# Scores and output projection of an attention and expert layer as plain fp32 products instead of three reduced ones

## What is computed

```python
# layer 0: attention, 16 heads of 64, one key/value head shared by all
xn = ln(x, g_norm)
q  = l2norm(heads(xn @ Wq)) * q_scale
k  = l2norm(concat([null_k, (xn @ Wkv)[..., :64]])) * k_scale
v  = concat([null_v, (xn @ Wkv)[..., 64:]])
sim  = einsum('bhid,bjd->bhij', q, k) * 8 + rel_pos_bias    # causal and mask
out  = einsum('bhij,bjd->bhid', softmax(sim), v)
x1   = x + ln(out.reshape(b, n, 1024) @ Wout, g_out)
# layer 1: 8 experts of width 128 (top 2) and a shared one of width 256
y = x1 + sum_k w_k * (leaky(x1 @ Wg_e) * (x1 @ Wu_e)) @ Wd_e + shared(x1)
```

## Time and profile before

| | before |
|---|---|
| time, median of 3 runs | 1070.17 us (1069.21 to 1070.3) |
| profiled execution | 1068.73 us, span 1066.9 us, mean TensorE clock 0.998 |
| TensorE busy | 1011.4 us (95%) |
| VectorE busy | 725.8 us (68%) |
| ScalarE busy | 541.0 us (51%) |
| GpSimd busy | 438.6 us (41%) |

### The profile page before, as it was taken

How to read it: one execution, slowest core, us unless ns; L and a number is a source line. 1 busy time by engine, 2 the same in 40 slices (tenths; PEclk the granted TensorE clock), 3 DMA queues, 4 the chain that set the end, 5 groups by cost and what they waited for, 6 DMA issues and landing times.

```text
span 1066.9 us, 22567 instructions
## 1 busy us (share of the span) xinstructions
PE 1011.4 (95%) x7300; PEld 823.6 (77%) x7300; DVE 725.8 (68%) x2497; ACT 541.0 (51%) x1596; POOL 438.6 (41%) x422
## 2 busy tenths in 40 slices
PE   3877999999999999999999999999999999999998
PEld 2765877878787887878777787787878788787877
DVE  8889487665867558665677647766586755866543
ACT  3598256652565435663456515665256643566220
POOL 1644254441454333642535515444145433354212
PEclk9999999999999999999999999999999999999999
DMA  5326423111132013311132212311113210221043
GB/s 198 73 77 209 138 69 121 51 60 62 61 110 89 36 47 100 100 61 61 42 114 77 69 42 72 119 49 62 62 61 110 89 37 29 96 103 62 36 133 105
DMA packets 41004, 87.79 MB, mean 82 GB/s; under 512 B 4193, under 2 KB 19041, under 8 KB 40625
## 3 DMA queue, kind: packets, MB, share of 16 engines
q1 hardware_dynamic: 39920, 83.57, 23.9%
q10 hardware_dynamic: 960, 2.62, 0.7%
HBM read 76.57 MB, written 9.60 MB: 81 GB/s over the span
## 4 chain that ended last, share of the span: by engine, by line
PE 70%; DVE 15%; issue 6%; ACT 3%; DVEq 0%; POOL 0%; ACTq 0%; POOLq 0%
PE psY L1647 13%; PE psS L1517 6%; PE psO L1553 5%; PE psG L71 5%; PE psG L69 5%; PE psG L70 5%; PE psT L1528 5%; PE psS L1512 3%; PE psS L69 2%; PE psS L71 2%; PE psS L70 2%; PE psT L1535 2%; PE psO L1556 2%; DVE work L423 2%; PE psT L69 2%
## 5 line engine op out<-in xcount | busy, mean ns | idle before, releaser
L592 POOL TENSOR_TENSOR work<-work,rden 128x514 f32<-128x514 f32 x128 | 134.2, 1049 | 328.6 <-DVE rden L1143 328.1
L1647 PE MATMUL psY<-Wd,H 128*128 128x256 f32 x640 | 171.7, 397 | 0.0
L757 ACT ACTIVATE work<-work,low 128x257 f32<-128x257 f32 x256 | 128.5, 504 | 63.5 <-DVE low L1161 63.5
L69 PE MATMUL psG<-x1T_hi,Wgu 128*128 128x512 f32 (+1 forms) x292 | 134.6, 461 | 3.5 <-ACT leaky L801 1.9
L1647 PEld LDWEIGHTS psY<-Wd,H 128*128 128x128 f32 x640 | 111.6, 189 | 28.1 <-issue 14.4
L1161 DVE CUSTOM_DVE_ANT_0 work<-psS,bias,null_s 128x256 f32<-128x256 f32 x256 | 113.1, 478 | 22.3 <-PE psS L1517 19.4
L1257 DVE SCALAR_TENSOR_TENSOR leaky<-leaky 128x512 f32<-128x512 f32 x80 | 55.4, 692 | 93.3 <-ACT leaky L801 93.3
L71 PE MATMUL psG<-x1T_lo,Wgu 128*128 128x512 f32 (+1 forms) x292 | 114.7, 393 | 0.0
L70 PE MATMUL psG<-x1T_hi,Wgu 128*128 128x512 f32 (+1 forms) x292 | 113.7, 389 | 0.0
L581 POOL TENSOR_TENSOR rq<-qss,neghalf 128x16 f32<-128x16 f32 x32 | 97.5, 3049 | 34.4 <-DVE qss L1137 34.4
L761 ACT ACTIVATE work<-work,low 128x129 f32<-128x129 f32 x256 | 99.4, 390 | 0.0
(11 more groups left out here) (264 smaller groups left out, 2567.6 us busy)
## 6 DMA issues: line engine op xcount, KB each, us to landing
Wgu<-wexp SPq DMA_DIRECT2D x80, 512.0 KB, 3.4
Wb<-wscr SPq DMA_DIRECT2D x64, 256.0 KB, 3.6
wexp<-Wgu SPq DMA_DIRECT2D x10, 512.0 KB, 2.9
xres<-in_x SPq DMA_DIRECT2D x8, 512.0 KB, 4.0
xin<-in_x SPq DMA_DIRECT2D x7, 512.0 KB, 4.1
out<-work SPq DMA_DIRECT2D x7, 512.0 KB, 3.2
H<-in_wgu SPq DMA_DIRECT2D x10, 256.0 KB, 3.5
bias<-bscr SPq DMA_DIRECT2D x4, 512.0 KB, 6.2
```

The costliest lines, as they stand in the source:

```text
L69: te.matmul(dst, a_hi, b_hi, start=start, stop=False)
L592: pool.tensor_tensor(T1[sl][:, hs, :], T1[sl][:, hs, :], rden[sl][:, 1, hs].unsqueeze(2) .to_broadcast([P, 2, N + 1]), ALU.mult)
L757: act.activation(T1[sl][:, h, :], T1[sl][:, h, :], ACT.Exp, scale=-1.0, bias=low[sl][:, 1, h:h + 1], accum_out=den[sl][:, 1, h:h + 1])
L1647: mm = te.matmul(psY[:, t // 2, (t % 2) * D:(t % 2 + 1) * D], H[:, k % H_RING, t * P:(t + 1) * P], Wd[:, ORDER[k], :], start=(k == 0 and t ...
```

## The change

Scores and the output projection become plain fp32 products. Queries, keys, head outputs and output weights are kept in one fp32 part each. The subtractions of the low parts go (`KB_lo`, `qT_lo` of queries and of head outputs, `wout_trail`), and so do the copies to `Wout_hi`. Of the eight units of turned queries ScalarE copies the even ones and VectorE the odd ones. The output weights are loaded straight to their place, and the residual of round 0 is loaded at the start, ahead of the down weights. The value product waits for ScalarE's copy (`o_lead`).

```diff
-        Wout = [sb(f"Wout_{part}", [P, PAIRS, D], F32R) for part in PARTS]
+        Wout = sb("Wout", [P, PAIRS, D])
-        KB = [sb(f"KB_{part}", [P, BB, N], F32R) for part in PARTS]
+        KB = sb("KB", [P, BB, N])
-        qT = [sb(f"qT_{part}", [P, PAIRS, TOK], F32R) for part in PARTS]
+        qT = sb("qT", [P, PAIRS, TOK])
...
+        def turned_q(eng, r, n):
+
+            t, half = n // 2, n % 2
+            need(eng, qT_ps, r, n + 1)
+            dst = qT[:, 4 * half:4 * half + 4, t * P:(t + 1) * P]
+            src = q_bank(n).rearrange("p (q i) -> p q i", q=4)
+            if half == 0:
+                eng.activation(dst, src, ACT.Copy).then_inc(qT_a.sem, 1)
+            else:
+                eng.tensor_copy(dst, src).then_inc(qT_v.sem, 1)
...
             sp.wait_ge(pre_v.sem, V_MASK)
-            load_mask(0)
+            load_round(0)
             sp.dma_start(Wd[:], wdown).then_inc(ld_down.sem, 16)
...
-            sp.wait_ge(pre_v.sem, V_WOUT)
-            sp.dma_start(xres[:], x_t[0]).then_inc(xres_in.sem, 16)
...
-            for half in range(2):
-                act.dma_start(Wout_in[half], wout[:, half * 4:half * 4 + 4, :]).then_inc(ld_out.sem, 16)
+            act.dma_start(Wout[:], wout).then_inc(ld_out.sem, 16)
...
-                for n in range(4):
-                    turned_q(r, n)
+                for n in (0, 2):
+                    turned_q(act, r, n)
...
-                    if moe is None and n in WOUT_AT:
-                        half = n - WOUT_AT[0]
-                        act.activation(Wout[0][:, half * 4:half * 4 + 4, :], Wout_in[half], ACT.Copy) \
-                            .then_inc(w_lead.sem, 1)
...
-                need(dve, kdT_ps, r, 1)
-                need(dve, kb_a, r, 1)
-                dve.tensor_tensor(KB[1][:, :, :], psO[:, :].rearrange("p (b j) -> p b j", b=BB),
-                                  KB[0][:, :, :].bitcast(F32), ALU.subtract).then_inc(kb_v.sem, 1)
...
-                for n in range(4):
-                    turned_q(r, n)
-                    if n == 0 and moe is not None:
-                        hidden(moe, 1)
-                    if n == 1 and moe is not None:
-                        router_weights(moe)
+                if moe is not None:
+                    hidden(moe, 1)
+                turned_q(dve, r, 1)
+                if moe is not None:
+                    router_weights(moe)
+                turned_q(dve, r, 3)
...
-                    if n >= VALUE_LAG:
-                        head_out(r, n - VALUE_LAG)
-                    for u in UNITS_AT.get(n, ()):
-                        turned_q(r, u)
+                    for u in UNITS_AT.get(n, ())[1:2]:
+                        turned_q(dve, r, u)
...
                     for p in range(PAIRS):
-                        products(te, dst, [part[:, p, t * P:(t + 1) * P] for part in qT],
-                                 [part[:, p, :] for part in Wout], p == 0, False)
+                        te.matmul(dst, qT[:, p, t * P:(t + 1) * P], Wout[:, p, :], start=(p == 0), stop=False)
...
                 for first, q1, keys_ in ((0, q0 + P, N), (N, q0, P)):
-                    for a, b in ((0, 0), (1, 0), (0, 1)):
-                        for i in range(2):
-                            half = slice(i * DH, (i + 1) * DH)
-                            mm = te.matmul(psS[:, i, first:first + keys_], qT[a][half, p, q1:q1 + P],
-                                           KB[b][half, bb, 0:keys_], start=False, stop=(first == N and b == 1))
+                    for i in range(2):
+                        half = slice(i * DH, (i + 1) * DH)
+                        mm = te.matmul(psS[:, i, first:first + keys_], qT[half, p, q1:q1 + P], KB[half, bb, 0:keys_],
+                                       start=False, stop=(first == N))
...
                 if n < LAST_VALUES:
-                    need(te, o_done, r, n)
+                    need(te, o_lead, r, n)
```

More of the change, by code:

```diff
@@ L50 @@
 FLIP_AHEAD = 2
-WOUT_AT = (3, 4)
 SPLIT_AT = 6
@@ L263, in attention_moe @@
         Wq_in = work[:, 0:KC * HEADS * DH].rearrange("p (c k) -> p c k", c=KC)
-        Wout_in = [half.rearrange("p (q d) -> p q d", q=PAIRS // 2) for half in
-                   (Wb[:, :, :].rearrange("p b t -> p (b t)"), xres[:, :, :].rearrange("p t d -> p (t d)"))]
         wprod = x1[:, :, :].rearrange("p t d -> p (t d)").rearrange("p (h d) -> p h d", h=HEADS)
@@ L347, in attention_moe @@
         kd_done = events("kd_done", 1)
-        kb_v = events("kb_v", 1)
         qss_done = events("qss_done", TILES)
         qn_done = events("qn_done", TILES - POOL_TILES)
-        qT_v = events("qT_v", 2 * TILES)
+        qT_v = events("qT_v", TILES)
         s1_read = events("s1_read", GROUPS * STEPS)
@@ L373, in attention_moe @@
         qs_done = events("qs_done", TILES)
-        qT_a = events("qT_a", 2 * TILES)
+        qT_a = events("qT_a", TILES)
         exp_done = events("exp_done", GROUPS * STEPS)
@@ L693, in attention @@
                         need(act, kdT_ps, r, 1)
-                        act.activation(KB[0][:, :, :], psO[:, :].rearrange("p (b j) -> p b j", b=BB),
+                        act.activation(KB[:, :, :], psO[:, :].rearrange("p (b j) -> p b j", b=BB),
                                        ACT.Copy).then_inc(kb_a.sem, 1)
@@ L705, in attention @@
                 for n in range(ALL + VALUE_LAG):
-                    for u in UNITS_AT.get(n, ()):
-                        turned_q(r, u)
+                    for u in UNITS_AT.get(n, ())[0:1]:
+                        turned_q(act, r, u)
                     if n == 1 and moe is not None:
@@ L738, in flipped @@
                     .then_inc(bias_done.sem, 1)
[L740 to L744, removed]
             def head_out(r, n):
@@ L950, in wall_trail @@
                                              Wall[0][:, c, a:b].bitcast(F32), ALU.subtract))
[L952 to L956, removed]
             dve.wait_ge(ld_rows.sem, 16)
@@ L1054, in attention @@
                         scale_q(dve, r, 3, qn_done)
-                    if moe is None and n - 1 in WOUT_AT:
-                        wout_trail(n - 1 - WOUT_AT[0])
-                    if n >= VALUE_LAG:
-                        head_out(r, n - VALUE_LAG)
-                    for u in UNITS_AT.get(n, ()):
-                        turned_q(r, u)
+                    for u in UNITS_AT.get(n, ())[1:2]:
+                        turned_q(dve, r, u)
                     if moe is not None and n in GATE_AT:
@@ L1114, in attention @@
                 cx.end()
[L1116 to L1122, removed]
             def null_parts(r):
@@ L1330, in null_products @@
                           stop=True).then_inc(pre_t.sem, 1)
-                te.wait_ge(ld_out.sem, 32)
+                te.wait_ge(ld_out.sem, 16)
                 for p in range(PAIRS):
-                    mm = te.matmul(psO[0:NULL_ROWS, 0:D], vn_cols[:, p, :], Wout_in[p // 4][:, p % 4, :],
+                    mm = te.matmul(psO[0:NULL_ROWS, 0:D], vn_cols[:, p, :], Wout[:, p, :],
                                    start=(p == 0), stop=(p == PAIRS - 1))
@@ L1381, in turn_q @@
                 else:
-                    need(te, qT_v, r, n - 3 if n < 6 else n - 1)
+                    need(te, qT_a if n % 2 == 0 else qT_v, r, 1 if n < 6 else 3)
                 for q in range(4):
@@ L1420, in attention @@
                 need(te, kb_a, r, 1)
-                need(te, kb_v, r, 1)
                 if moe is not None:
@@ L1437, in attention @@
                     if n == 0:
-                        need(te, qT_a, r, 4)
-                        need(te, qT_v, r, 4)
+                        need(te, qT_a, r, 2)
+                        need(te, qT_v, r, 2)
                     if n < ALL:
@@ L1463, in attention @@
                     if n == TURN_LAG:
-                        need(te, qT_a, r, 2 * TILES)
-                        need(te, qT_v, r, 2 * TILES)
+                        need(te, qT_a, r, TILES)
+                        need(te, qT_v, r, TILES)
                     if TURN_LAG <= n < ALL + TURN_LAG:
@@ L1471, in attention @@
                     turn_x(following)
-                need(te, o_done, r, ALL)
+                need(te, o_lead, r, ALL)
                 need(te, s1_read, r, ALL)
@@ L1545, in value @@
                 if n < LAST_VALUES:
-                    need(te, o_done, r, n)
+                    need(te, o_lead, r, n)
                 else:
-                    need(te, o_done, r, n - 1)
+                    need(te, o_lead, r, n - 1)
                     if moe is not None:
```

11 lines of the change are left out of this document (2 added, 9 removed).

## The result

The changed kernel takes 1077.13 us (median of 4 runs, 1076.73 to 1077.51) against 1069.69 before (1068.92 to 1070.3): a ratio of 1.0074, 95% interval 1.0059 to 1.0089. It is slower by about 7.5 us, where the forecast was slower by 2.

The account below looks back on a forecast made before the run. TensorE bounds most time, VectorE some 17 us of each attention loop, ScalarE and VectorE round 0. Products +19.2 +3.8, less 0.3 hidden, 14.7 and 6.0 back: +2.2, 1072 us against the median; range 1061 to 1092.

Parts of the forecast that it names:

- Output projection, +19.2: TensorE, 32 tiles: eight plain products take 3.45 us instead of 2.85 for the reduced ones, +0.60 a tile, +19.2 us.
- Scores, +3.8: TensorE, 128 score steps: two pairs of plain products replace six reduced pairs, +0.03 us a step, +3.8 us.
- Rival A: Score products: halves do not overlap on 64 rows; 1084 to 1098 us, or 1154 if nothing overlaps; chance 0.18 for both.
- that rival's smaller form: Scores: each half's second pass must start before the other's first; 0.1 to 0.2 us a step, 13 to 26 us.
- Loop rounds, 2.1 back a round: Rounds 1 to 7: TensorE's waits return 2.1 us a round against 2.4 projection and 0.5 scores, net +5.6 us.
- VectorE binds: 1.8 back: Up to the third score step (420.05): three query/key subtractions gone bring VectorE 1.8 us forward; TensorE could use about 2.0.
- the 0.3 at 470.94, where 0.42 a step is gone: Late in a loop round: TensorE's wait before a mask's product returns 0.3 us as head-output subtractions of 0.42 go.
- Round 0, 6.0 back: Round 0: 3.0 us from ScalarE copies, 1.7 and 1.3 from VectorE subtractions return; less 2.4 and 0.2, net -3.4 us.
- B: Rival: all TensorE waiting behind 403 returns, 3.1 us a round, and round 0 gives 9; 1062 us, chance 0.27.
- C: Rival: only half of the 2.1 and 6.0 returns, as a gate's copy or router chain takes the place; 1082, chance 0.13.
- The waits at the mask's product: Sign: TensorE's waits before score mask products, 0.77 at 415.76, 0.86 at 420.05, 0.23 at 470.94, gone or under 0.3.
- the stretch behind 403: Part of each loop round where TensorE waits; the prediction fails if this stretch keeps its waits.

Follow-up runs that it names:

- the two pairs of kernels: Changed kernel against the relief alone (1077.13 and 1057.08 us); the products alone against the kernel before (1089.52 and 1069.69 us).
- The run in four parts: Changed kernel with VectorE's 2.1 us normalization of the following x given out one tile a step over steps 11 to 14: 1073.53 us, ratio 1.0047.
- the products alone: Kernel before with plain products in scores and projection, every copy and subtraction of the other engines kept: 1089.52 us, ratio 1.0195.
- the relief alone: Changed kernel with lighter VectorE and ScalarE, but TensorE's products as before in number and type: 1057.08 us, ratio 0.9888.

## Why the prediction was right, and where its sizes were off

**Output projection, +19.2:** right. 3.46 a tile by the chain instead of 2.85, 0.6 x 32; the run with the plain projection alone has rounds 2.43 us longer, where 2.4 was the term. The count by four passes that the Trainium skill gives ("FP8 and Floating Point Precision", TensorE Precision Notes) would make +30, an estimate at 0.119 a pass; the trace does not agree with it as a price: a plain product is worth 3.6 reduced ones of 256 columns, since a reduced one takes 0.119 and not a fourth of 0.43.

**Scores, +3.8:** right in kind, somewhat too much. Thirteen steps grew by 0.13 to 0.16 us together, 0.01 a step, some 1.5 us in all. The forecast had added 0.02 a step for the wider weight loads, and nothing of it shows. Rival A is out for the order that the change uses: the two heads' plain products overlap on 64 rows as the value products do on 64 columns. The other order costs 0.11 a step, the size of that rival's smaller form, but not in the way it said: there the second head's 256-column passes start ahead of the first head's 128-column ones. The Trainium skill ("TensorE: Matmul & The Clock Gate", Part 3, What overlaps and what doesn't) has matmuls start and end in strict program order. By the starts in the profile the trace does not agree: in the run with the other order all four 256-column passes start before the first 128-column one, in all 128 steps. Whether the order was changed in the array or before it, no run shows.

**All products:** 23.0 worked out, 19.9 and 20.9 measured by the two pairs of kernels.

**Loop rounds, 2.1 back a round:** the mis-sized term. With plain products the mean round lost 129.21 - 127.76 = 1.45 (0.52 ahead of the first score, 0.98 at the first two steps, nothing later), and with reduced ones 126.57 - 125.33 = 1.24. Two steps of the working failed.

The first is "VectorE binds: 1.8 back" up to the third score step; 1.50 came, or 1.38 with reduced products, and TensorE could have used 2.0. The working took VectorE's queue for a block that only gets shorter. The queue contains a wait for ScalarE, which in turn waits for VectorE's first read, and this ring has a length of its own. The run with the leaky step moved gives the missing 0.53, and the run with the scaling moved shows that the load is not the cause.

The second is "the 0.3 at 470.94, where 0.42 a step is gone". Nothing of it came: that wait is for a piece of 2.1 us that lies between two score reads, and a lighter step elsewhere does not shorten it. The run in four parts shows it. Together the two are 0.65 a round, 4.6 us over seven, or 0.86 and 6.0 with reduced products.

**Round 0, 6.0 back:** too much, by half. About 3 came back: 3.3 at the full clock in both (113.1 with the products alone, 109.8 with the program of the change), and 3.0 at 0.97 in both (114.1 before, 111.1 with the relief alone). These are single executions. The term had counted each microsecond taken from ScalarE or VectorE in full. Six copies put back on ScalarE brought 3.1 to 4.0 of their 5.7, so by estimate the 3.0 taken from ScalarE was worth about 2. Which part of VectorE's 3.0 was lost, and to which engine, is open; no run took it apart.

**How much was luck.** The sign and the range held, but the forecast was a small difference, 2 us, of two large sums, 23 and 21. The products came out 2 to 3 us cheaper than worked out and the relief 8 to 9 us smaller. The first error covered part of the second; without it the time would have been near 1080. The range of 31 us was wide enough to hold either sign of the change.

**Rivals B and C.** B (all waits come back) is out: the waits for ScalarE stayed, as the prediction had it. What came true lies between the forecast and C: 12 to 13 us of relief where 20.7 was worked out, 10 to 11 in C. Its reason, that a gate's copy takes the place, is what happened at the third score step.

**The signs.** A tile of 3.9 us, 0.65 for the score passes: seen. VectorE "near 645": 660.3, since whole durations were taken for busy time. The waits at the mask's product "gone or under 0.3": so at one place and at the last one, where it had been under 0.3 before; 0.47 is left at the third score step. Round 0 some 6 us earlier: 2.7. Of its signs of failure, a score step 0.1 longer did not come. Round 0 giving less than 3 is met by the 2.7 and just missed by the 3.0 and 3.3 above, and the stretch behind 403 kept part of its waits (0.27 and 0.47). So by its own signs the two relief terms were in doubt. The start cost nothing, as counted: the null product begins at 22.40 instead of 22.73.

## What to carry to other kernels

Where one engine is full, price its products from rows of the same type and shape, and the rest of a change only by the waits of that engine. When an engine ahead of such a wait looks full, follow its queue item by item: if one item waits for a third engine that waits for the first, the load is not the bound and taking work out gives only part; moving one item out of the ring gave 0.53 us a round here, beside the 0.98 that all the removed work gave at the same steps. And of two edits made together, try each alone: here the plain scores gave 7.4 us and the plain projection cost 17.

## What was not expected of the hardware

Eight plain passes on two halves of 64 rows took 0.65 us when the heads alternate in the program and 0.76 when one head's products come first, one 128-column pass more; and in that order the second head's 256 columns started ahead of the first head's 128. The granted clock of TensorE stood at half for a short stretch of round 0 in some executions and not in others: two executions whose program is the same up to there ended the round at 109.8 and at 111.4 us, while rounds 2 to 6 of the changed kernel agree to 0.1 us.
